# Cross attention: half of each tile's probabilities turned by VectorE in 32x32 squares and moved by DMA

## The reference

```
kv_rope = kv_c * cos[None] + _rotate_half(kv_c) * sin[None]
...
scores = jnp.einsum('bshr,bhlr->bhsl', q_r, k_r)
attn = jax.nn.softmax(scores, axis=-1)
ctx_c = jnp.einsum('bhsl,bld->bhsd', attn, kv_rope)
```

## Time and profile before

| | us |
|---|---|
| median of 3 runs (3444.37 to 3445.53) | 3444.7 |
| the profiled execution's own time | 3440.74 |
| its span, first to last instruction | 3438.9 |
| TensorE busy over the span | 3190.4 (93%) |
| VectorE, ScalarE, GpSimd busy | 1711.5, 1381.0, 490.6 |
| mean granted clock of TensorE, share of full speed | 0.962 |

### The profile page before, as it was taken

How to read it: one execution, slowest core, us unless ns; L and a number is a source line. 1 busy time by engine, 2 the same in 40 slices (tenths; PEclk the granted TensorE clock), 3 DMA queues, 4 the chain that set the end, 5 groups by cost and what they waited for, 6 DMA issues and landing times. The chain is left out here.

```text
span 3438.9 us, 57532 instructions
## 1 busy us (share of the span) xinstructions
PE 3190.4 (93%) x22977; PEld 2103.5 (61%) x22981; DVE 1711.5 (50%) x3608; ACT 1381.0 (40%) x2348; POOL 490.6 (14%) x362
## 2 busy tenths in 40 slices
PE   4899999996999989999999999989999999768999
PEld 3667777774445553577777656763577777536444
DVE  5445555543232247666666233347666666464222
ACT  3345556531111132466666222222466666333221
POOL 4212122100216014200000000004200000202000
PEclk8899999997999999999999999999999999988999
DMA  1222222211222212112221110012112221100111
GB/s 30 68 77 53 59 63 49 63 41 44 96 70 94 87 29 78 34 41 52 50 50 38 47 31 27 24 35 80 35 41 53 49 50 38 33 11 22 32 37 36
DMA packets 195497, 167.43 MB, mean 49 GB/s; under 512 B 90260, under 2 KB 166022, under 8 KB 192784
## 3 DMA queue, kind: packets, MB, share of 16 engines
q1 hardware_dynamic: 195232, 163.76, 17.4%
HBM read 120.46 MB, written 21.23 MB: 41 GB/s over the span
## 5 line engine op out<-in xcount | busy, mean ns | idle before, releaser
L1727 ACT ACTIVATE l0x_shared<-l0x_shared,l0x_a_low 128x1500 f32<-128x1500 f32 x112 | 173.3, 1547 | 191.1 <-DVE l0x_shared L1683 188.8
L1727 ACT ACTIVATE l1x_shared<-l1x_shared,l1x_a_low 128x1500 f32<-128x1500 f32 x112 | 173.1, 1545 | 188.6 <-DVE l1x_shared L1683 188.6
L1727 ACT ACTIVATE l2x_shared<-l2x_shared,l2x_a_low 128x1500 f32<-128x1500 f32 x112 | 173.1, 1545 | 188.6 <-DVE l2x_shared L1683 184.3
L1618 PE MATMUL l0x_a_T_ps<-ident,l0x_shared 128*125 128x128 f32 x1344 | 176.1, 281 | 15.3 <-issue 14.7
L1618 PEld LDWEIGHTS l0x_a_T_ps<-ident,l0x_shared 128*125 128x125 f32 x1344 | 155.1, 187 | 39.4 <-issue 37.4
L1618 PE MATMUL l1x_a_T_ps<-ident,l1x_shared 128*125 128x128 f32 x1344 | 176.5, 281 | 0.8 <-ACT l1x_shared L1727 0.8
L1618 PE MATMUL l2x_a_T_ps<-ident,l2x_shared 128*125 128x128 f32 x1344 | 176.5, 281 | 0.8 <-ACT l2x_shared L1727 0.8
L1602 PE MATMUL l0x_a_S_ps<-l0x_kt,l0x_a_q 64*128 64x375 f32 x896 | 173.3, 505 | 2.7 <-DMA l0x_a_q<-l0x_qa 2.7
L1618 PEld LDWEIGHTS l2x_a_T_ps<-ident,l2x_shared 128*125 128x125 f32 x1344 | 155.2, 187 | 29.8 <-issue 28.2
L1618 PEld LDWEIGHTS l1x_a_T_ps<-ident,l1x_shared 128*125 128x125 f32 x1344 | 155.1, 187 | 29.8 <-issue 28.2
L1602 PE MATMUL l2x_a_S_ps<-l2x_kt,l2x_a_q 64*128 64x375 f32 x896 | 172.1, 501 | 0.5 <-DVE l2x_shared L1683 0.5
(11 more groups left out here) (654 smaller groups left out, 6004.8 us busy)
## 6 DMA issues: line engine op xcount, KB each, us to landing
l0f_gu<-in_L_ffn_gu SPq DMA_DIRECT2D x36, 256.0 KB, 2.6
l0x_a_q<-l0x_qa SPq DMA_DIRECT2D x64, 96.0 KB, 2.9
l1x_a_q<-l1x_qa SPq DMA_DIRECT2D x64, 96.0 KB
l2a_w<-in_L_attn_qkv SPq DMA_DIRECT2D x16, 384.0 KB, 3.1
l2x_a_q<-l2x_qa SPq DMA_DIRECT2D x64, 96.0 KB, 2.3
l0x_raw<-in_ctx SPq DMA_DIRECT2D x16, 375.0 KB
kv_rotated<-l0x_v SPq DMA_DIRECT2D x16, 375.0 KB
kt_rotated<-l0x_kt SPq DMA_DIRECT2D x16, 375.0 KB, 4.7
```

The source lines that it names most:

```text
L1618: last = pe.transpose(T_ps[0:KP, g, kk * 128:(kk + 1) * 128], p[:, n % 2, j % HJ // 3 * 2 + j // HJ, j % 3 * KP:(j % 3 + 1) * KP], m.ident[:])
L1727: act.activation(p[:, n % 2], p[:, n % 2], ACT.Exp, bias=low[:, n % 2, 1:2], scale=-1.0, accum_out=den[:, b % 2, k:k + 1]).then_inc(exp_re ...
```

## The change

The 1,500 keys are cut anew: six blocks of 128 (KD) and six of 122 (KP), instead of twelve of 125. The 122 blocks go as before, through TensorE (six transposes a tile, into two banks, both now copied by ScalarE). The 128 blocks, 768 columns, are turned by VectorE (`block_turn`), which turns each square of 32 x 32 in its place; it takes the place of VectorE's `keep`. What is left is to move whole squares between groups of 32 partitions: sixteen transfers (`move`) for each of two groups of tiles, four and three tiles, a batch. Each is 32 partitions of 3,072 bytes (first group) or 2,304 (second), from SBUF to SBUF, issued by SyncE. The values go in the same two groups, 256 and 192 columns, in seven pieces, so that a batch's last five pieces lie in the next batch's tiles. Rotated values get a third buffer in the first layer, keys and values are fetched by separate steps in the others, the queries lie tile by tile (four transfers of 64 partitions), and the inverses' fetch is two transfers. Around these stands a new order of SyncE's list. The layout of the context and its tables on the host follows the new cut.

```diff
-KP, KJ = 125, 12
+KD, KP, KJ = 128, 122, 6
...
-    UNIT = (0, 0, 1, 1, 2, 2, 2)
-    COLS = ((0, 128), (128, 256), (256, 448))
-    PARTS = {1: (0, 0), 2: (0, 6), 3: (1, 0), 5: (1, 6), 6: (2, 0), 7: (2, 6)}
+    FIRST, COUNT = (0, 4), (4, 3)
+    W1, W2, JB = 3 * KD, 3 * KP, KJ * 32
+    PIECES = {5: (0, 0, 3), 6: (0, 3, 6), 7: (0, 6, 9), 8: (0, 9, 12), 9: (1, 0, 4), 10: (1, 4, 8), 11: (1, 8, 12)}
...
+        moved_to, blocks, at = [], [], KJ * C
+        for g, space_ in enumerate((m.normed[:, 0:4 * COUNT[0] * JB], st.sb(name + "blocks", [128, 4 * COUNT[1] * JB])[:])):
+            moved_to.append(space[:, at:at + 4 * COUNT[g] * JB].rearrange("k (q t j b) -> k q t j b", q=4, t=COUNT[g], j=KJ))
+            blocks.append(space_.rearrange("q (l t j b) -> q l t j b", l=4, t=COUNT[g], j=KJ))
+            at += 4 * COUNT[g] * JB
...
-        T_ps = st.ps(name + "T_ps", [128, 3, 512])
-        C_ps = st.ps(name + "C_ps", [128, 2, 256])
+        T_ps = st.ps(name + "T_ps", [128, 2, 512])
+        C_ps = st.ps(name + "C_ps", [128, 2, 512])
...
-                        lane = slice(to * CW, (to + 1) * CW)
-                        source = qa[half, b % HALF].rearrange("c o h s -> c o (h s)")
                         for odd in range(2):
-                            sp.dma_start(q[lane, b % 2, 0:768].rearrange("c (i o n) -> c i o n", i=3, o=2)[:, :, odd],
-                                         source[:, odd, 0:384].rearrange("c (i n) -> c i n", i=3)).then_inc(q_loaded[b % 2], 16)
-                        sp.dma_start(q[lane, b % 2, 768:896].rearrange("c (o n) -> c o n", o=2),
-                                     source[:, :, 384:448]).then_inc(q_loaded[b % 2], 16)
+                            sp.dma_start(q[to * CW:(to + 1) * CW, b % 2].rearrange("c (t o s) -> c t o s", t=T, o=2)[:, :, odd],
+                                         qa[half, b % HALF, odd].rearrange("c h s -> c (h s)").rearrange("c (t s) -> c t s", t=T)
+                                         ).then_inc(q_loaded[b % 2], 16)
 
...
+                def move(b, g):
+
+                    sp.wait_ge(blocked, T * b + FIRST[g] + COUNT[g])
+                    if b > 0:
+                        sp.wait_ge(valued, 2 * (b - 1) + g + 1)
+                    for l in range(4):
+                        for qi in range(4):
+                            sp.dma_start(moved_to[g][32 * l:32 * l + 32, qi].rearrange("k t j b -> k (t j b)"),
+                                         blocks[g][32 * qi:32 * qi + 32, l].rearrange("q t j b -> q (t j b)")
+                                         ).then_inc(moved[g][b % 2], 16)
...
-                        whole = m.r_dram[b, 0:6].rearrange("(i o) q -> o i q", o=2)[odd]
-                        sp.dma_start(rrow[lane, j, 0:384].rearrange("c (i q) -> c i q", i=3),
-                                     whole.partition_broadcast(CW)).then_inc(r_loaded[j], 16)
-                        sp.dma_start(rrow[lane, j, 384:448], m.r_dram[b, 6, lane].partition_broadcast(CW)).then_inc(r_loaded[j], 16)
+                        sp.dma_start(rrow[lane, j].rearrange("c (t s) -> c t s", t=T),
+                                     m.r_dram[b][:, lane].partition_broadcast(CW)).then_inc(r_loaded[j], 16)
...
                     fetch_queries(b)
                 if ctx is not None:
                     store_values(0)
+                    store_values(1)
+                    ahead.fetch_context(sp, 2)
                     store_keys(0)
                 for b in range(B):
-                    if ctx is not None and b + 1 < B:
-                        store_values(b + 1)
-                        if b + 2 < B:
-                            ahead.fetch_context(sp, b + 2)
-                        store_keys(b + 1)
+                    move(b, 0)
                     if b + 2 < B:
                         sp.wait_ge(scored, 2 * (T * b + 6) + 2)
                         fetch_queries(b + 2)
+                        if ctx is None:
+                            ahead.fetch_keys(sp, b + 2)
+                    if ctx is None and 0 < b < B - 1:
+                        sp.wait_ge(valued, 2 * b)
+                        ahead.fetch_values(sp, b + 1)
+                    if ctx is not None and b + 2 < B:
+                        store_values(b + 2)
+                    if ctx is not None and b + 3 < B:
+                        ahead.fetch_context(sp, b + 3)
+                    if ctx is not None and b + 1 < B:
+                        store_keys(b + 1)
+                    move(b, 1)
                     if b + 1 < B:
                         store_inverses(b)
-                    if ctx is None and b + 2 < B:
-                        sp.wait_ge(valued, 3 * b + 3)
-                        ahead.fetch_keys(sp, b + 2)
-                    if b + 1 < B:
                         fetch_inverses(b)
...
                 def turn(n):
                     pe.wait_ge(exp_ready, n + 1)
...
+                    for g in range(2):
                         if n > 0:
+                            pe.wait_ge(pt_kept, 2 * (n - 1) + g + 1)
+                        for k in range(3):
+                            j = 3 * g + k
+                            at = 2 * W1 + j % 2 * W2 + j // 2 * KP
+                            last = pe.transpose(T_ps[0:KP, g, k * 128:(k + 1) * 128], p[:, n % 2, at:at + KP], m.ident[:])
+                        last.then_inc(turned, 1)
...
+                def values(b, g, first, end):
...
+                    for j in range(first, end):
+                        if j == KJ:
+                            pe.wait_ge(moved[g][b % 2], 256 * (b // 2 + 1))
+                        for odd in range(2):
+                            out = C_ps[odd * CW:(odd + 1) * CW, g, 0:z - a]
+                            if j < KJ:
+                                last = pe.matmul(out, v[0:KP, b % nv, KJ + j, :], pt[:, j, odd, a:z], start=(j == 0), stop=False)
                             else:
+                                r, i = (j - KJ) // 3, (j - KJ) % 3
+                                last = pe.matmul(out, v[:, b % nv, 2 * i + r, :],
+                                                 moved_to[g][:, 2 * odd:2 * odd + 2, :, j - KJ, :].rearrange("k q t b -> k t q b"),
+                                                 start=False, stop=(j == 2 * KJ - 1))
...
+                    if k > 4:
+                        values(b, *PIECES[k])
+                    elif b > 0:
+                        values(b - 1, *PIECES[k + T])
...
-                            dve.wait_ge(turned, 3 * (n - 2) + 3)
+                            dve.wait_ge(turned, 2 * (n - 2) + 2)
+                            dve.wait_ge(blocked, n - 1)
...
+                def block_turn(n):
+
+                    b, k = n // T, n % T
+                    g = group(k)
+                    dve.wait_ge(exp_ready, n + 1)
+                    if b > 0 and k == FIRST[g]:
+                        dve.wait_ge(moved[g][(b - 1) % 2], 256 * ((b - 1) // 2 + 1))
+                    dve.transpose(blocks[g][:, :, k - FIRST[g]].rearrange("q l j b -> q j l b"),
+                                  p[:, n % 2, 0:2 * W1].rearrange("q (j l b) -> q j l b", j=KJ, l=4)).then_inc(blocked, 1)
...
-                def keep(n):
-
-                    b, k = n // T, n % T
-                    dve.wait_ge(turned, 3 * n + 1)
...
                 for n in range(N):
...
+                    block_turn(n)
                     invert(n)
-                    keep(n)
                     if n + 2 < N:
                         negate(n + 2)
...
+                    for g in range(2):
+                        act.wait_ge(turned, 2 * n + g + 1)
+                        act.copy(pt[:, 3 * g:3 * g + 3, :, k * 64:(k + 1) * 64],
+                                 T_ps[0:KP, g, 0:W1].rearrange("k (j o q) -> k j o q", j=3, o=2)).then_inc(pt_kept, 1)
```

More of the change, by code:

```diff
@@ L1381, in fetch @@
                 self.fetch_keys(sp, b)
+                self.fetch_values(sp, b)
             else:
@@ L1442, in attend @@
         turned = st.sem(name + "turned")
-        pt_dve = st.sem(name + "pt_dve")
-        pt_act = st.sem(name + "pt_act")
+        pt_kept = st.sem(name + "pt_kept")
+        blocked = st.sem(name + "blocked")
+        moved = [[st.sem(f"{name}moved{g}{j}") for j in range(2)] for g in range(2)]
         rden_ready = st.sem(name + "rden_ready")
+        pt_used = st.sem(name + "pt_used")
         valued = st.sem(name + "valued")
@@ L1579, in turn_keys @@
                     if b > 0:
-                        pe.wait_ge(pt_dve, n + 1)
-                        pe.wait_ge(pt_act, 2 * n + 1)
-                    for i in range(HJ):
-                        last = pe.transpose(T_ps[:, i // 3, i % 3 * KP:(i % 3 + 1) * KP],
-                                            v[:, b % 2, i].rearrange("p a e -> p (a e)"), m.ident[0:KP, 0:KP])
+                        pe.wait_ge(pt_kept, 2 * n + 2)
+                    for i in range(KJ):
+                        k = KD if i < 3 else KP
```

(51 more changed lines are left out.)

183 lines of the change are left out of this document (91 added, 92 removed).

## The result

The changed kernel takes 3683.3 us (3676.8 to 3690.6) against 3445.0 before: 1.069 times as long, interval 1.068 to 1.071. It is slower by 238 us. The profiled execution took 3690.6 us (span 3688.3), 249.9 more than the one before; it is the longest of the four, 7.3 us above their median.

The account below looks back on a forecast made before the run. SyncE's in-order queue bounds, at 36.7 us a batch. Layers gain 75.2 and twice 94.6, sum +264.4 on the profiled 3440.74, 3705, plus 4.0 for the median: 3709 us; range 3340 to 3770, likeliest case 3640 to 3780.

Parts of the forecast that it names:

- The bound: SyncE's in-order queue sets the batch at 36.7 us, against TensorE's 25.2 and the old 30.8.
- three signs: In the queue: no wait for blocks, 8.8 us between store and fetch; VectorE and TensorE waiting once a batch, 11 us.
- The queue's batch: SyncE's list per batch: 32 moves at 0.65 plus 15.9 us for the rest, 36.7 us; 37.2 in the first layer.
- c: Price of issuing one move of 32 partitions within SBUF on SyncE's queue, taken as 0.65 us from the queries.
- Rival B: Same SyncE queue, but 32 partitions issue like 128 in series, 0.47 us a move: 3431 us, chance 0.27.
- The wait: SyncE waits 8.84 us per batch for the inverses' store to land before their fetch; the next moves stand behind it.
- Rival D: The store of the inverses lands in 2 us, so a batch falls to 29.9 us: 3403 us, chance 0.02.
- the rule of 2 us: Trainium skill's fixed DMA cost, about 2 us from issue to completion whatever the size; would make the queue's batch 6.8 shorter.
- TensorE's tile: TensorE's work per tile after the change: 0.75 transposes, 1.46 scores, 1.38 values, 3.59 us; 25.2 a batch.
- rival C: Moves issue at 0.37 us or less: 3277 us; below 0.29 TensorE is the bound, 3188 us. Chance 0.17.
- VectorE's transpose: VectorE's new SBUF to SBUF transpose of 768 columns replacing its copy: taken as 0.86 us, upper bound 1.7.
- The clock: TensorE at 1.2 GHz after waits: hidden by 11.5 us of idling within a batch, 2 to 4 at each layer's end.

Follow-up runs that it names:

- The best version: Changed kernel with inverses fetched after the next batch's first moves, ScalarE issuing their store and a quarter of moves, second group's moves before later loads: 3270.0 us, ratio 0.951.

## Why the prediction was right, and where its steps were off

It said slower, 3709 us; 3683 was measured, and the profiled executions differ by 249.9 where its sum had 264.4. So 14.5 of the 26 us are in the layers; the other 11 come from adding the old kernel's step from the profiled execution to the median, +4.0, where the changed kernel's is −7.3.

- **The bound** was named rightly: SyncE's queue. Its three signs are there: no wait for the blocks, 8.8 us between store and fetch, TensorE and VectorE waiting once a batch. TensorE also had a second, shorter wait in most batches, for the second group (18.6 of its 123.6 us). The doubled moves change the time by what the queue's sum says (4675 us for 4660); the moved fetch and the store in rows take 327 us each, where it says 386 and 283.
- **The queue's batch**: 36.7 us forecast, 36.1 measured from move to move, 35.9 from the first fetch of the second layer to its last (503.2 / 14); 37.2 forecast and measured in the first. The layers came out as 596.1, 578.1 and 578.4 for 594.3 and twice 586.8. The surplus of 8.5 in two of them is the queue's, 15 × 0.6 = 9.
- **c**, the term that decided: a move issues in 0.59, 0.63 from start to start, and 0.66 with the overruns counted in, for 0.65 + 0.04. 32 × 0.03 is 1.0, more than the whole 0.6; against it stands the store, put at 0.45 and measured at 0.62 with its gap, though the same paragraph has a row of it behind another transfer at 0.59. The queries were the right neighbour, and two reasons were given for them: that they are the only transfers within SBUF, which the runs bear out, and that they "cover whole quarters of the partitions but not all", which they don't. "Size does not order these rows, the number of partitions does" failed: 128 partitions within SBUF cost 0.61. That the value held in spite of this rule is in part luck. Rival B, 32 priced like 128 in series, took its 0.47 from transfers with DRAM at one end, and had no ground in that form.
- **The wait**: 8.84 forecast, 131 us over 15 times in each layer, 8.75. Rival D rested on the rule of 2 us; the rows spoke against it rightly, and only with rows of 28 bytes does the store land near that, in 1.7. The cure was nearer than any rival saw: the fetch can come after the next batch's first moves, and no engine that sets the time waits for it.
- **TensorE's tile**: 3.59 forecast, 3.71 measured. Six transposes take 0.80 instead of 0.75, and the pieces of values 1.45 instead of 1.38. The products that read in runs of 32 elements take 1.51 us a piece, like the others beside them, so such reads cost nothing visible. So the floor of rival C is 26.0 a batch, not 25.2, and its 3188 us would have been near 3250: 4 × 3.1 + 108 × 3.71 + 13 after the last transposes = 426 for a layer, where rival C had 406.5. The best version's 433.8 is 8 above that.
- **VectorE's transpose**: 0.97 for 0.86, inside its bounds, and it never decided. The first tiles without values come every 3.1 us, as forecast. The Trainium skill (Vector Engine (DVE) Microarchitecture Reference, The reshape front-end and per-opcode configuration) has the 32 x 32 transpose pipelined to sustain one element per cycle per lane. The trace agrees so far as that it is no slower than VectorE's other single passes: 768 columns in 0.97 stand beside the passes of 768 columns from PSUM in 0.96.
- **The clock**: left in the range, and it hides behind the queue while batches run. It does lift TensorE's busy share to 78% where "some 70%" was forecast: seven tiles of 3.71 in 36.1 us are 72%, and most of the rest is work after the waits that takes nearly twice as long, 2.83 us for 1.51. Its waits are 8.8 us a batch (123.6 / 14) for the 11 forecast.

## What to carry to other kernels

Before transfers are put on a queue that works in order, add up the whole list per period: every issue at its own price and every wait for a landing, those too that cost nothing so far. A wait that was free behind a slower engine becomes part of the period as soon as work that matters stands behind it; here one line moved later gave back more than the change had lost. If the queue is then still the bound, only fewer or cheaper issues help, or a second issuing engine: ScalarE's share of the moves took 41 us, and the order of one queue without a pause changed nothing that could be measured. Once the queue stands idle at times and an engine still waits, the order inside the period counts, and what is needed soonest goes first: another 25 us here.

## What the runs showed of the hardware

- SyncE issues a transfer within SBUF in 0.59 to 0.65 us, in series, at 32, 64 or 128 partitions and, at 32, at half or all of the bytes; after a pause a move takes 0.51. With DRAM at one end and 32 or 128 partitions it takes 0.31 to 0.37 after a pause, and at 128 partitions 0.58 to 0.63 right behind a transfer within SBUF. ScalarE issues moves at 0.55 to 0.61 in the median, beside its running exponential. GpSimd takes 0.50 each as busy time.
- Right behind four transfers of four times a move's bytes a query's issue takes 1.26 us in the median, behind moves 0.65.
- A stage in which GpSimd issued DMAs ended 10.5 us later, six times of six.
- 896 words of 4 bytes into DRAM land in 9.2 us, the same words as 128 rows in 1.7.
- The DMA engines' busy share is no measure of the data moved: 0.58 at 146 GB/s with the inverses in rows, 0.81 at 147 with single words and the fetch moved, 0.74 at 214 through DRAM.
- Issues run over now and then, single ones by 1 to 6 us: a move's mean with them, gap included, is 0.66 in the changed kernel's second layer, 0.69 with the fetch moved, and 0.74 with the fetch moved and GpSimd issuing beside SyncE. Taking the word-wise store out of that queue did not stop it. What causes it stays open.
